# Last step of both LayerNorms as an activation between the seventh and eighth exponential, attention slots written out

## The reference

```python
def _layernorm(x, axis=-1, eps=1e-05):
    m = jnp.mean(x, axis=axis, keepdims=True)
    v = jnp.var(x, axis=axis, keepdims=True)
    return (x - m) / jnp.sqrt(v + eps)
...
    x = x + _L0_xattn_ref(_layernorm(x, axis=-1), ctx_1024, ctx_1024, mask_BxS2_bf0, ...)   # 16 heads of 8
    x = x + _L0_ffn_ref(_layernorm(x, axis=-1), L0_ffn_Wr, ...)                             # top 2 of 8 experts, 512 hidden
```

## Time and profile before

| | |
|---|---|
| median of 3 runs | 1009.66 us (1009.06 to 1009.77) |
| the profiled execution, its own time | 1012.47 us |
| its span in the trace | 1010.7 us |
| attention slots in the span | 0 to about 700 us |
| busy: PE, DVE, ACT, POOL | 81%, 70%, 54%, 49% |
| chain that ended last, shares of the span | PE 49%, DVE 19%, issue 13%, DMA 9%, SPq 5%, POOL 3%, ACT 2% |

### The profile page before, as it was taken

How to read it: one execution, slowest core, us unless ns; L and a number is a source line. 1 busy time by engine, 2 the same in 40 slices (tenths; PEclk the granted TensorE clock), 3 DMA queues, 4 the chain that set the end, 5 groups by cost and what they waited for, 6 DMA issues and landing times.

```text
span 1010.7 us, 22541 instructions
## 1 busy us (share of the span) xinstructions
PE 822.4 (81%) x5927; PEld 595.5 (59%) x5927; DVE 706.6 (70%) x2191; ACT 550.4 (54%) x1005; POOL 492.9 (49%) x672
## 2 busy tenths in 40 slices
PE   3887899879879978979978988851999999999900
PEld 2555565656556556656655655630888888888700
DVE  6645778767868868868768877643577777777736
ACT  5534455545545545544545554331888888888700
POOL 5333444435434534534534455354177777767730
PEclk9778899989989999989999998885899999999955
DMA  5444443223323323422323344465877777777249
GB/s 152 104 115 116 125 135 95 69 69 96 81 63 99 89 63 79 101 71 67 96 68 83 91 113 116 115 242 175 261 236 240 247 247 243 236 244 247 86 142 356
DMA packets 136613, 143.34 MB, mean 142 GB/s; under 512 B 19884, under 2 KB 101143, under 8 KB 135512
## 3 DMA queue, kind: packets, MB, share of 16 engines
q1 hardware_dynamic: 117672, 119.18, 42.0%
q0 software_dynamic: 9088, 17.07, 4.8%
q10 hardware_dynamic: 9776, 6.29, 2.0%
HBM read 72.61 MB, written 36.08 MB: 108 GB/s over the span
## 4 chain that ended last, share of the span: by engine, by line
PE 49%; DVE 19%; issue 13%; DMA 9%; SPq 5%; POOL 3%; ACT 2%; DVEq 1%; POOLq 0%; ACTq 0%
DVE mx L677 7%; PE bank L1231 5%; PE bank L1405 4%; PE bank L1407 3%; PE bank L1243 3%; PE bank L1406 3%; PE bank L1393 3%; PE bank L1390 3%; PE bank L1391 3%; PE bank L1221 3%; DMA kb<-ks 3%; DMA qb<-negm 3%; DVE yy L687 3%; DMA qb<-yd 2%; PE bank L1179 2%
## 5 line engine op out<-in xcount | busy, mean ns | idle before, releaser
L607 POOL DMA_INDIRECT yd<-vs,idt x156 | 164.6, 1055 | 85.7 <-DVE vs L973 45.9
L1038 ACT ACTIVATE pt<-bank 120x512 f32<-120x512 f32 x256 | 145.6, 596 | 92.4 <-PE bank L1231 90.7
L677 DVE TENSOR_REDUCE mx<-bank 128x4 f32<-128x480 f32 x256 | 159.9, 647 | 37.6 <-PE bank L1221 37.6
L522 POOL DMA_INDIRECT xd<-rows,posi x128 | 129.1, 1009 | 110.0 <-DVE posi L752 64.3
L953 DVE TENSOR_TENSOR qb<-hid,qb 128x512 fp32r<-128x512 f32 x156 | 109.5, 702 | 71.0 <-ACT hid L1130 69.7
L1221 PE MATMUL bank<-kb,qs 128*128 128x480 f32 x256 | 104.5, 454 | 41.0 <-DVE mx L677 22.0
L1231 PE MATMUL bank<-qb,ks 128*120 128x512 f32 x256 | 124.3, 507 | 7.4 <-DMA qb<-negm 7.2
L1127 ACT ACTIVATE qb<-bank,btile 128x512 fp32r<-128x512 f32 x156 | 107.6, 690 | 34.0 <-PE bank L1407 25.7
L1243 PE MATMUL bank<-pt,vs 120*32 120x128 f32 x2048 | 113.8, 296 | 5.1 <-ACT pt L1038 4.2
L1130 ACT ACTIVATE hid<-bank,btile 128x512 f32<-128x512 f32 x156 | 106.3, 682 | 0.0
L1221 PEld LDWEIGHTS bank<-kb,qs 128*128 128x128 f32 x256 | 48.7, 200 | 82.0 <-DVE mx L677 56.9
(11 more groups left out here) (200 smaller groups left out, 2101.2 us busy)
## 6 DMA issues: line engine op xcount, KB each, us to landing
kb<-wd SPq DMA_DIRECT2D x40, 512.0 KB, 5.2
qb<-wd SPq DMA_DIRECT2D x38, 512.0 KB, 5.0
qb<-qs SPq DMA_DIRECT2D x128, 128.0 KB
kb<-ks SPq DMA_DIRECT2D x128, 120.0 KB
rows<-xd SPq DMA_DIRECT2D x39, 264.0 KB, 2.8
wd<-wsp SPq DMA_DIRECT2D x8, 1024.0 KB, 5.3
qb<-yd SPq DMA_DIRECT2D x16, 512.0 KB, 5.6
xd<-zrows SPq DMA_DIRECT2D x8, 528.0 KB, 3.7
```

What stands on the lines that cost most here:

```text
L522: g.indirect_dma_start(xd, bass.IndirectOffsetOnAxis(ap=posi[r.phase][:, bk:bk + 1], axis=0), rows[r.phase][:, bk // 2, bk % 2, :], None, ...
L607: g.indirect_dma_start(yd, bass.IndirectOffsetOnAxis(ap=idt[k][:, j:j + 1], axis=0), yrow[p.parity][:, j, :], None, bounds_check=2 * NTOK ...
L677: v.tensor_reduce(mx[:, b, gg, :], wide[(4 + u) % 3][:, 0:J * KL].rearrange("p (j k) -> p j k", j=J), op=ALU.max, axis=AX.X).then_inc(w_fr ...
L1038: a.activation(pt[t % NP][:].rearrange("p j q -> p (j q)"), scores[t % 2][0:KL, :], ACT.Exp, scale=SCALE).then_inc(exp_done, 1)
```

## The change

It does two things.

First, `slots` no longer has a loop: all 36 slots are written out on all five engines, and what was computed in registers is now a constant.

Second, the last step of both LayerNorms, `(x - mean) * y`, leaves VectorE. VectorE computes a further column, `shift = mean * -1 * y`, directly behind `y`, for which it waits (so `LN`, the number of counts of `ln_chain` per slot, is 7 and no longer 6). ScalarE then does `Identity(scale * x + bias)` with `y` as scale and `shift` as bias: in slot n two activations for `rows` (chunk n-1) and two for `xn` (chunk n+3), all four between its seventh and eighth exponential. The first `xn` stands ahead of all slots. The waits of `norm_x` and `norm_x1` go along to ScalarE.

```diff
         def slots(eng, body):
-            for s in range(-2, 4):
-                body(At(s // 4, s % 4), s)
-            with eng.Fori(1, NCH // 4 - 1) as quad:
-                for phase in range(4):
-                    body(At(quad, phase), None)
-            for s in range(NCH - 4, NCH + 2):
+            for s in range(-2, NCH + 2):
                 body(At(s // 4, s % 4), s)
...
-                        last = v.scalar_tensor_tensor(ys[1][:, :], vyy[:, :], 1.5, ys[0][:, :], ALU.add, ALU.mult)
+                        v.scalar_tensor_tensor(ys[1][:, :], vyy[:, :], 1.5, ys[0][:, :], ALU.add, ALU.mult).then_inc(ln_chain, 1)
+                        dve.wait_ge(ln_chain, (s + 3).count(LN, 6))
+                        last = v.scalar_tensor_tensor(shift[:, :], mv[:, :, 0], -1.0, ys[1][:, :], ALU.mult, ALU.mult)
...
-                    if u == 4:
-                        norm_x1()
...
-                norm_x()
...
                     if t == 6:
+                        if exists(n, -1):
+                            m = s + -1
+                            act.wait_ge(ln_chain, (s + 3).count(7, 7))
+                            if exists(n, -2):
+                                act.wait_ge(x2t_full, s.count(1, -1))
+                            if exists(n, -5):
+                                act.wait_ge(scat[m.phase], m.turns(64, -64))
+                            for b in range(2):
+                                last = a.activation(rows[m.phase][:, b, 0, 0:D], xres[:, 2 * n - 2 + b, :], ACT.Identity,
+                                                    bias=shift[:, 2 + b:3 + b], scale=ys[1][:, 2 + b:3 + b])
+                            last.then_inc(ln2_done, 1)
+                        if exists(n, 3):
+                            norm_x(s, n)
                         exponentials(s, 7, n)
...
+            def norm_x(s, n):
+                f = s + 3
+                act.wait_ge(ln_chain, f.count(7, 7))
+                if exists(n, 1):
+                    act.wait_ge(tx_full, s.count(1, 2))
+                for b in range(2):
+                    last = a.activation(xn[f.parity][:, b, :], xres[:, 2 * n + 6 + b, :], ACT.Identity,
+                                        bias=shift[:, b:b + 1], scale=ys[1][:, b:b + 1])
+                last.then_inc(lnx_done, 1)
...
+            norm_x(At(-1, 1), -3)
             slots(act, slot)
```

More of the change, by code:

```diff
@@ L132, in moe_attention @@
         yy = sb("yy", [P, 4])
+        shift = sb("shift", [P, 4])
         vyy = sb("vyy", [P, 4])
@@ L526, in root @@
             def root(s):
-                alone(pool, ln_chain, (s + 3).count(6, 3))
+                alone(pool, ln_chain, (s + 3).count(7, 3))
                 g.tensor_tensor(ys[0][:, :], ve[:, :], minus_half[:, :], ALU.pow).then_inc(root_done, 1)
@@ L655, in slot @@
                 k = c.parity
-                LN = 6
+                LN = 7
                 if exists(n, 1) and (n is None or n >= 1):
@@ L752, in position @@
                         v.tensor_copy(posi[r.phase][:, :], posf[:, :]).then_inc(pos_done, 1)
-                def norm_x():
-                    if exists(n, 3):
-                        f = s + 3
-                        dve.wait_ge(ln_chain, (s + 3).count(LN, 6))
-                        if exists(n, 1):
-                            dve.wait_ge(tx_full, s.count(1, 2))
-                        for b in range(2):
-                            last = v.tensor_scalar(xn[f.parity][:, b:b + 1, :], xres[:, bass.ds(f.count(2, b), 1), :],
-                                                   mv[:, b, 0:1], ys[1][:, b:b + 1], ALU.subtract, ALU.mult)
-                        last.then_inc(lnx_done, 1)
-                def norm_x1():
-                    if exists(n, -1):
-                        m = s + -1
-                        dve.wait_ge(ln_chain, (s + 3).count(LN, 6))
-                        if exists(n, -2):
-                            dve.wait_ge(x2t_full, s.count(1, -1))
-                        if exists(n, -5):
-                            dve.wait_ge(scat[m.phase], m.turns(64, -64))
-                        for b in range(2):
-                            last = v.tensor_scalar(rows[m.phase][:, b:b + 1, 0, 0:D], xres[:, bass.ds(m.count(2, b), 1), :],
-                                                   mv[:, 2 + b, 0:1], ys[1][:, 2 + b:3 + b], ALU.subtract, ALU.mult)
-                        last.then_inc(ln2_done, 1)
                 if n == 0:
```

## The result

| | before | after |
|---|---|---|
| median, both run side by side | 1009.71 us (4 runs) | 965.09 us (963.83 to 966.29, 4 runs) |
| ratio, 95% interval | | 0.9556 (0.954 to 0.9573) |
| the profiled execution | 1012.47 us | 964.7 us |
| its span | 1010.7 us | 962.9 us |

The forecast was 967 us in a range of 957 to 982. The largest terms were right; the term for the start was wrong in sign, and the one for the end was too large.

What follows compares the result with a forecast made beforehand. Bound: VectorE's stalls at five loop turns and a chain through `y`, maxima, transpose, `negm`, its DMA and scores. 1012.47 - 31 - 15.8 + 2.4 + 0.8 + 0.5 = 969.4, against the median 967 us; range 957 to 982.

Steps and rivals of the forecast that it cites:

- The sum: Whole kernel: all terms added to the profiled execution of 1012.47 us give 969.4, or 967 us against the median shown.
- The turns: Five turns of the attention loop, where VectorE stalls: writing slots out saves 6.2 us each, -31 us; bounds 24.9 and 31.
- Rival D: VectorE's stall belongs to every fourth slot, not the loop's branch, so it stays: 998 us; chance 0.02.
- Registers: Waits on the slot's chain (`xcT` to `xcTl`, `negm` to DMA issue) compare with constants: 0.36 us a slot saved.
- `rows`, -0.30: Second LayerNorm's pair off VectorE: last maximum ready earlier, TensorE's transpose of `mx` starts 0.30 us earlier in each slot.
- `xn`, nothing: First LayerNorm's pair off VectorE: counts nothing, since `rden` behind it needs TensorE's transposes.
- `shift` and the activations: Added VectorE product (0.2 us) and four ScalarE activations (0.45 each less 0.1 overlap) are covered in ordinary slots: nothing.
- rival B: ScalarE late: activations of 0.69 us each hold `onT` behind exponential 8, 0.4 us a slot: 977 us; chance 0.07.
- Straight code stalls (C): Written-out slots stall for new code, say 2.5 us a slot: 1027 us, slower; chance 0.03, taken as nothing.
- The start: Slots -2 and -1: `xn` ahead of ScalarE's clearing of tiles delays the start by 1.6 to 3.2 us, taken +2.4.
- the first slots with weights: Slots 0 to 3, sharing +0.8 us with 28 to 31: `shift` lacks VectorE cover where GpSimd's `wsp` holds `y`.
- The last slots: End of the attention part: `shift` and slower activations lie on the chain, +0.5 us.

Runs made afterwards that it cites:

- hint: Kernel before with a back-edge hint on VectorE's loop of slots, nothing else changed; median 1018.5 us, 0.9825 of before on that chip.
- body8: Kernel before with eight slots in the loop's body on every engine, two turns in place of five; 1021.3 us, 0.9831 of before on that chip.
- written: Kernel before with all slots written out, LayerNorms left on VectorE; run twice: 1009.3 us (0.973 of before on that chip) and 1015.6 us (0.9638).
- mixed: Kernel after with slots written out for VectorE and ScalarE alone, TensorE, GpSimd and SyncE in the loop; 1016.7 us, 0.9662 of before on that chip.
- rows_back: Kernel after with the second LayerNorm's step (`rows`) back on VectorE behind the fifth maximum; 982.8 us, 0.973 of before.
- xn_back: Kernel after with the first LayerNorm's step (`xn`) back on VectorE at the slot's end; 966.8 us, 0.9564 of before.
- ln_loop: Kernel before with its loop kept and both LayerNorms' last steps on ScalarE; 1028.4 us, 0.9873 of before on that chip.
- act_twice: Kernel after with four more like activations on ScalarE ahead of the eighth exponential in slots 4 to 23; 984.3 us, 0.9737 of before.
- later: Kernel after with the square root's small steps and the first of the position one maximum later in each slot; 951.4 us, 0.9413 of before.
- mixed_later: Kernel after, slots written out for VectorE and ScalarE alone, small square-root steps one maximum later; 990.3 us, 0.9341 of before on that chip.

## Why the prediction was right, and where it was wrong

**The sum.** It was made for the profiled execution, 969.4 us, and that came to 964.7. Of the 4.7 us between them the start is 3.9 (+2.8 forecast with half of the 0.8, -1.1 measured), the last slots are 0.6 (+0.9 and +0.3) and the expert part, for which nothing was forecast, is 1.6; the 24 slots gave 1.4 less than forecast. That the median missed by 1.9 only is luck: before, the profiled execution was 2.8 us above the median shown, and after, it was 0.4 below.

**The turns, -31.** Right: 30.9 measured as 467.42 less 24 times 18.19 (30.4 of it in the five slots over a turn), and 30.5 in hint, where nothing else changed. Of the bounds, 24.9 and 31, the upper was it. The reason given, a fetch of code, is borne out by the vanished packets in hint and by TensorE's new stall in body8. Rival D is out: hint and body8 keep each fourth slot's work and lose the stall there.

**Registers, -0.36 a slot.** Right in size: hint to written is 18.17 to 17.81, and the hold of `yy` shortens by the same 0.36. Right in place: mixed keeps GpSimd, SyncE and TensorE in the loop, and both pieces are back.

**`rows`, -0.30; `xn`, nothing.** Measured 0.34 by written against after and by rows_back; xn_back gives 0.01. The two terms don't add in any order, though: in the loop the LayerNorm's move gave 0.13 (ln_loop), and with it made, leaving GpSimd, SyncE and TensorE in the loop costs 0.49 (mixed). The prediction read both terms from the loop's trace and took them as independent. That their sum, 0.66, met 0.72 is in part luck, since in the loop alone the second was worth 0.13.

**`shift` and the activations, nothing.** Right; two activations in a row take 0.88 us of ScalarE's time, against 0.45 taken for one, less 0.1 of overlap. The estimate by the Trainium skill, ScalarE: Activation LUTs, What ACT_TABLE_LOAD costs, was 0.48 for one; with the same overlap two are 0.86, and the trace agrees. The cover was taken too large (1.3 for about 0.66, by act_twice), since it was read from the weighing and not from `onT`, which the forecast named as queued there and only rival B gave a price.

**Straight code stalls (C), taken as nothing.** This is the step that failed in kind. No wait on issue of that kind came on VectorE, but packets of instructions meet narrow transfers on the chain. Against each kernel's undisturbed slot the odd ones cost 2.9 us in after, 5.8 and 10.0 in the two runs of written and 7.3 in later; with TensorE in a loop and q8 quiet, 0.1 are left (mixed_later). The prediction looked for waits on VectorE only; the place to look was a DMA. GpSimd has one wait on issue of over 0.5 us in these slots; every kernel with GpSimd's slots written out has one near that place, of 2.2 to 4.0 us, and none with them in a loop:

```profile
213.53 0.97 POOL L518 DMA_INDIRECT xd<-rows,posi  x1 [3.20 <-issue]
```

Its slot takes 17.50 us, so this costs nothing here; what it waits for isn't shown. By the Trainium skill, Runtime: NRT & Kernel Launch, Instruction fetch mechanics, straight code is fetched ahead; the trace of after agrees in that VectorE, ScalarE and TensorE have no wait on issue in the view of waits, and shows the price elsewhere.

**The start, +2.4, and the first slots with weights, half of +0.8.** The start was late as worked out: the first `part` at 19.88 (forecast 20.5), the one of the next slot 2.77 late.

```profile
19.88 1.18 ACT L1000 ACTIVATE part<-bank,rowselk 128x480 fp32r<-128x480 f32 x2
...
36.90 1.19 ACT L1000 ACTIVATE part<-bank,rowselk 128x480 fp32r<-128x480 f32 x2
```

But the lateness did not last. Two `negm`, three slots apart, of after and then of before:

```profile
56.56 0.28 DVE L826 SCALAR_TENSOR_TENSOR negm<-bank,negm 32x128 fp32r<-32x128 f32 x1
...
123.77 0.28 DVE L826 SCALAR_TENSOR_TENSOR negm<-bank,negm 32x128 fp32r<-32x128 f32 x1
```

```profile
53.21 0.28 DVE L856 SCALAR_TENSOR_TENSOR negm<-bank,negm 32x128 fp32r<-32x128 f32 x1
...
124.85 0.28 DVE L856 SCALAR_TENSOR_TENSOR negm<-bank,negm 32x128 fp32r<-32x128 f32 x1
```

3.35 us late at the first, 1.08 early at the second. In the first of the three TensorE waits for `kb`, after and before:

```profile
69.86 1.17 PE L1214 MATMUL bank<-kb,qs 128*128 128x480 f32 x2 [3.13 <-DMA kb<-ks]
```

```profile
67.12 1.17 PE L1221 MATMUL bank<-kb,qs 128*128 128x480 f32 x2 [4.45 <-DMA kb<-ks]
```

1.32 us of the lateness went into this wait. In the next slot it waited 1.47 us for `negm` before and 0.30 after. Over the three slots its waits for transfers come to 12.65 us before and 10.98 after, 1.67 less. `rows` off VectorE, which the prediction counted in the 24 slots alone, may give another 1.0 (three times 0.34); 1.7 of the 4.43 regained has no account. In xn_back, where `xn` isn't late, the same `negm` stand at 54.08 and 124.06: 2.5 us ahead of after at the first, 0.3 behind it at the second. The failed step is that a lateness ahead of slots which wait 2 to 5 us for a transfer was carried to the end as if they had no slack.

**The last slots, +0.5 and the other half of +0.8.** The last three slots took 66.1 us, against 65.8 before, so +0.3 of it is there. The remaining 1.6 us of gain lie in the expert part (351.0 against 352.6), which the change doesn't touch; in the four other kernels of a chip where the kernel before took 1009 us it took 350.5 to 353.4.

## What to carry to other kernels

A loop's turn can cost an engine several microseconds (6.2 here) when its body is long; look for a wait on issue at the turn and for instruction packets in the list of queues, and try the back edge's hint before writing the loop out, since the written-out slots here paid in packets that meet narrow transfers. A freed instruction is worth the wait of whoever waits for it next and no more. Carry a lateness only as far as the next slots that wait for something else.

## What the runs showed of the hardware

- With the hint, VectorE's loop needed no instruction packet at all in 345 us, where 25 had moved; I had expected them earlier, not gone. Whether the hint or a shift of the body's place kept it whole was not tried.
- Packets of q8 are 16 KB (0.70 MB in 43), of q14 8 KB (0.39 MB in 47). q8 falls silent when TensorE runs in a loop of four slots; behind one of them a wait for `negm` of 1.76 us was seen, where about 0.15 or none is usual.
- A wait of TensorE of 0.99 or 1.76 us is followed by about 8 us at a clock of 0.79 in the mean; waits of 1.02 and 1.41 us passed without it.
- VectorE's `yy` ends as GpSimd's `xcTl` ends wherever it starts within it: it takes 1.21 us in most slots of the loop, 0.85 in most of after, 0.29 in most of later.
